# The last two transposes of a unit in the outputs' PSUM bank, in a fused attention and FFN block

## The reference

```python
x = L0_attn_hidden_states            # (4, 512, 1024)
xn = _layernorm(x, axis=-1)
x = x + attn(xn, w_qkv, w_o) + ffn(xn, W, b, A, B, gate_w, gate_b)

# attn: 32 query heads, 8 key/value heads, D = 128
scores = jnp.einsum('bqhgd,bkhd->bhgqk', q, k) * scale
bias = -slopes[:, :, None, None] * sqrt_dist          # -inf above the diagonal
attn = jax.nn.softmax(scores + bias[None], axis=-1)
out = jnp.einsum('bhgqk,bkhd->bqhgd', attn, v)
return out.reshape(B, S, NH * D) @ w_o
```

## Time and profile before

| | |
|---|---|
| median of 3 runs | 2472.68 us (2472.03 to 2477.65) |
| profiled execution, its own time | 2475.28 us |
| its span in the trace | 2473.4 us |
| PE busy | 2377.9 us (96%) |
| DVE busy | 1547.1 us (63%) |
| ACT busy | 1373.4 us (56%) |
| POOL busy | 784.2 us (32%) |
| granted TensorE clock, mean | 0.991 |

### The profile page before, as it was taken

The page is one execution under the profiler, slowest core; times in us unless marked ns, Lnnn a source line. Parts: engine busy times, 40 slices in busy tenths (PEclk is TensorE's granted clock), DMA queues, the critical chain, the costliest instruction groups (busy, mean ns, idle before and its releaser), DMA issues.

```text
span 2473.4 us, 34303 instructions
## 1 busy us (share of the span) xinstructions
PE 2377.9 (96%) x11616; PEld 1991.7 (81%) x11616; DVE 1547.1 (63%) x2969; ACT 1373.4 (56%) x3051; POOL 784.2 (32%) x1029
## 2 busy tenths in 40 slices
PE   5999999998799999999899999999999999999999
PEld 4787888887678788888778888788888888888887
DVE  5657355655655645555676666767667666676665
ACT  4532133334533223333477777777777777777774
POOL 3211000000330100000244645446455464554644
PEclk9999999999899999999999999999999999999999
DMA  4536445546254635445655565655655556666553
GB/s 151 182 129 209 146 146 184 191 170 236 71 175 157 207 120 204 153 170 196 235 185 182 188 230 203 208 194 188 226 201 210 198 188 218 201 211 206 187 175 141
DMA packets 118318, 455.90 MB, mean 184 GB/s; under 512 B 11945, under 2 KB 12089, under 8 KB 109184
## 3 DMA queue, kind: packets, MB, share of 16 engines
q1 hardware_dynamic: 86176, 334.37, 39.2%
q0 software_dynamic: 31968, 119.33, 13.9%
HBM read 276.96 MB, written 176.69 MB: 183 GB/s over the span
## 4 chain that ended last, share of the span: by engine, by line
PE 85%; DVE 5%; ACT 4%; issue 3%; DMA 3%; POOL 1%; SPq 0%; ACTq 0%; DVEq 0%; POOLq 0%
PE ps L677 26%; PE ps L678 26%; PE ps L679 26%; PE ps L877 5%; DMA lora_lo<-lora_s 1%; DMA qk_s<-res_b 1%; ACT probs L1085 1%; ACT res_hi L945 1%; DVE stats L1197 1%; DVE wo L1183 1%; ACT rows L974 1%; PE ps L857 1%; ACT probs L1107 1%; DVE w_lo L1183 0%; DMA qk_s<-res_hi 0%
## 5 line engine op out<-in xcount | busy, mean ns | idle before, releaser
L945 ACT ACTIVATE w_hi<-raw 128x1024 fp32r<-128x1024 f32 x196 | 207.0, 1059 | 558.9 <-PE ps L679 439.5
L1467 DVE TENSOR_TENSOR acc<-ps,acc 128x512 f32<-128x512 f32 x448 | 297.2, 686 | 287.3 <-issue 260.8
L1183 DVE TENSOR_TENSOR w_lo<-raw,w_hi 128x1024 fp32r<-128x1024 f32 x196 | 239.1, 1224 | 357.8 <-ACT w_hi L945 357.6
L677 PE MATMUL ps<-x_hi,w_hi 128*128 128x512 f32 x1120 | 436.5, 390 | 0.0
L678 PE MATMUL ps<-x_lo,w_hi 128*128 128x512 f32 x1120 | 436.0, 389 | 0.0
L679 PE MATMUL ps<-x_hi,w_lo 128*128 128x512 f32 x1120 | 435.9, 389 | 0.0
L1085 ACT ACTIVATE probs<-probs,neg_max 128x512 f32<-128x512 f32 (+3 forms) x512 | 283.9, 566 | 168.8 <-DVE neg_max L1432 168.8
L677 PE MATMUL ps<-wo,op_hi 128*128 128x512 f32 x896 | 363.5, 406 | 2.0 <-POOL op_lo L635 0.7
L678 PE MATMUL ps<-wo,op_hi 128*128 128x512 f32 x896 | 352.1, 393 | 0.0
L679 PE MATMUL ps<-wo,op_lo 128*128 128x512 f32 x896 | 351.5, 392 | 0.0
L679 PEld LDWEIGHTS ps<-x_hi,w_lo 128*128 128x128 f32 x1120 | 210.4, 188 | 43.9
(11 more groups left out here) (166 smaller groups left out, 4637.1 us busy)
## 6 DMA issues: line engine op xcount, KB each, us to landing
raw<-w_all SPq DMA_DIRECT2D x70, 1024.0 KB, 5.4
q<-qk_s SPq DMA_DIRECT2D x128, 512.0 KB, 3.9
acc<-acc_s SPq DMA_DIRECT2D x128, 512.0 KB, 5.1
acc_s<-acc SPq DMA_DIRECT2D x112, 512.0 KB, 7.7
qk_s<-res_hi POOLq DMA_DIRECT2D x40, 1024.0 KB, 4.6
qk_s<-res_a POOLq DMA_DIRECT2D x20, 1024.0 KB, 9.2
qk_s<-res_b POOLq DMA_DIRECT2D x20, 1024.0 KB, 5.2
k<-qk_s SPq DMA_DIRECT2D x32, 512.0 KB, 3.6
```

The lines of the kernel that those rows point to most:

```text
L677: pe.matmul(to, st_hi, mv_hi, start=start, stop=False, skip_group_check=True)
L945: nc.scalar.activation(to, source, ACT.Copy).then_inc(signal, 1)
L1183: nc.vector.tensor_tensor(to, source, high.bitcast(F32), ALU.subtract).then_inc(signal, 1)
L1467: nc.vector.tensor_tensor(to, fill[f % 2][:, :], to, ALU.add).then_inc(s_acc, 1)
```

## The change

The third group of transposes goes to `ps_o` instead of `ps_c`. The wait of that group for the maxima of the next unit's widest scores is taken out, and so is the wait of the widest scores for the copies of the transposes two units back. Nothing else differs; the same instructions run on every engine in the same order.

```diff
@@ -170,8 +170,7 @@
         score_rest = ps_a[:, P:2 * P]
         SCORES = (3, 2, 1, 0)
 
-
-        t_banks = [(ps_t0, 0, 512), (ps_t1, 512, 512), (ps_c, 1024, 256)]
+        t_banks = [(ps_t0, 0, 512), (ps_t1, 512, 512), (ps_o, 1024, 256)]
         o_banks = [ps_o, ps_t1]
 
         s_ident = sem("s_ident")
@@ -848,8 +847,6 @@
                 for c, i in enumerate((3, 2, 0, 1)):
                     if n and i != 1:
                         pe.wait_ge(s_neg_max, QT * (n - 1) + (c + 1 if i else 4))
-                    if n >= 2 and i == 3:
-                        pe.wait_ge(s_pt_lo, 3 * (n - 1))
                     cut, keys = slice(i * P, (i + 1) * P), slice(0, (i + 1) * P)
                     if i == 0:
 
@@ -871,8 +868,6 @@
                         [(0, i) for i in range(4)], [(1, 1), (1, 2), (1, 3), (3, 3)], [(2, 2), (2, 3)])):
                     if to is ps_t1 and n >= 2:
                         pe.wait_ge(s_at_raw, n // 2)
-                    if to is ps_c and n + 1 < UNITS:
-                        pe.wait_ge(s_neg_max, QT * (n + 1) + 1)
                     for c, (j, i) in enumerate(blocks):
                         last = pe.transpose(to[:, c * P:(c + 1) * P],
                                             probs[:, n % 2, OFF[i] + j * P:OFF[i] + (j + 1) * P], ident[:, :])
```

## The result

| | before | after |
|---|---|---|
| median of 8 runs each, us | 2473.52 (2471.59 to 2477.65) | 2480.91 (2479.24 to 2482.96) |
| ratio, 95% interval | | 1.0029 (1.0018 to 1.0040) |
| profiled execution, us | 2475.28 | 2480.64 |
| its span, us | 2473.4 | 2478.8 |
| mean granted clock of it | 0.991 | 0.989 |

The change made the kernel 7.4 us slower, clear of noise. The median lies over the range that was forecast (to 2477.5) and just under its bound of 0.3% for "slower".

What follows compares the result with a forecast made beforehand. PE, busy 96% of the span, was taken to bound the kernel, so only standing time could be gained. All parts were taken as 0: profiled 2475.3 us, median about 2472.5 us, range 2468.5 to 2477.5 us; no change got 0.93.

Steps and rivals of the forecast that it cites:

- its bound of 0.3% for "slower": Whole kernel: about 0.3%, 7.4 us, is what a measurement can tell from no change; slower than that got 0.04.
- Part one, the transposes' wait: Attention stage, ahead of the third group: wait removed, but the third fill still waits for DVE's addition; gain 0.
- The rival that gains 20.9 us: PE's attention-stage waits: both removed waits are gained whole, 19.1 + 1.8 us, giving 2451.8 us; chance 0.03.
- Part two, the scores' wait: Scores waiting for `pt_lo`, 1.79 us in step 6: the wait moves to that step's transposes; gain 0.
- Parts three and four, queue and bank: PE's queue: some 250 fewer waits, 0 to 2.5 us off, taken as 0; `ps_o` bank: over 3 us spare, cost 0.
- Part five, the clock: Turns of the output weights: joined waits could change clock falls, 1.22 us each; no change taken.
- possible better case: Turns of the output weights: the fill now ahead of the wait makes clock falls less frequent, 1.2 us faster.
- the worse one: Turns of the output weights: the joined 2.3 us wait brings up to 6 more clock falls, 7.3 us slower.
- the rival that had it: Turns of the output weights: the joined wait lets the clock fall at each, 2480 to 2490 us; chance 0.04.
- The argument against: Against the slower-clock rival: waits of 1.79 and 1.18 us within 7 us in step 6 brought no clock fall.

Runs made afterwards that it cites:

- the split run: Changed kernel, with PE waiting for the first maximum between the second fill's two products in steps with n % 16 == 6: 2475.89 us, ratio 1.0008.

## Why the prediction was wrong, point by point

- **Part one, the transposes' wait: right.** The third fill starts when it did in relation to the maxima (2.67 us both times); the wait became 1.05 us in the odd steps and 2.11 to 2.16 us in the even ones. The forecast was 1.22 and 2.30 us, reckoned from start to start; so reckoned, steps 37 and 38 of the changed kernel have 1.23 and 2.30 us. A turn without a fall takes 155.24 us after and 1713.68 - 1558.39 = 155.29 us before. The rival that gains 20.9 us is dead.
- **Part two, the scores' wait: right**, by the run that put it back (2480.95 beside 2480.91 us).
- **Parts three and four, queue and bank: right at 0.** The run with the new bank and only the transposes' wait put back equals the kernel before (1.0001, 0.9992 to 1.0010). So the new bank and one wait instruction fewer in each step cost and bring nothing that can be measured.
- **Part five, the clock: this is the step that failed.** The prediction had the mechanism and its price and wrote "I take no change": it took the total standing time as deciding and let a possible better case weigh against the worse one. The runs showed 5 falls at 7 turns in place of 1. The price was sized too low as well, 1.22 us against 1.44 us: it was read from the third fill alone, and in the changed kernel the slow stretch reaches into the outputs behind it. 0.04 was given to the rival that had it. Its lowest figure, 2480 us, is near the 2480.91 us measured by a different sum: it took a fall of 1.22 us at every turn, and there were five of seven, each dearer.
- What should have turned it: step 22 of the kernel before, one fall behind 1.82 us of waiting, said that the turns stood near the edge, and near an edge a change of the spacing need not be neutral. The argument against, that 1.79 and 1.18 us in step 6 brought no fall, spoke of pieces no longer than those that already were there, and not of one of over 2 us.
- The range left out its own rival. It took in three more falls of 1.2 us; five of seven at 1.44 us went past it.
- **The Trainium skill's rule.** The prediction cited the Trainium skill, "TensorE: Matmul & The Clock Gate", Part 4, that a transpose doesn't count as busy for the gate in the way a matmul does. By that rule it would have been 1.2 us faster. The runs don't bear it out: there were more falls, not fewer, and twenty-six transposes in a row, with 0.4 us of the 2.1 us of standing left behind the next fill, had the clock at 1.00 at every turn. Here they count for something, and with that the reason for the better case falls: in the kernel before, the wait was a piece of 1.8 us and not one of over 3 us with the transposes around it.

What stays open: why a fall comes at some turns and not at others of the same execution, and how standing time in two pieces adds up; the split run shows only that both happen. It is not shown either that the joining is the reason for the four falls more: the change made one piece longer and also moved it behind the second fill. The longest piece alone doesn't decide, since pieces of 0.93 and 0.96 us brought three falls where the kernel before, with one of 1.83 us, has one.

## What to carry to other kernels

When an edit only moves a wait on a TensorE that is the bound, the sum isn't zero by itself: look at the granted clock behind each place where it stands, and if one of several equal places already shows a fall, price the case in which all do. A wait that interrupts work early can be worth more than the same wait later in one longer piece; better still is to follow the wait to the engine that is late, here a 1.4 us split in DVE's order that had itself waited 1.8 us for ACT, and whose move gave 14 us. And a wait in the list is a gain only if what comes next isn't waiting for the same engine: the next signal of that engine tells.

## What the runs showed of the hardware

- One piece of 2.1 to 2.2 us without PE work in a dense stream was followed by the 1.2 GHz level for some 3.4 us at 5 of 7 places, in each of two kernels; one of 1.8 us at 1 of 7, in each of two kernels; two of 0.93 and 0.96 us at 3 of 7; one of some 1.43, 0.80 or 0.39 us at none. Each count is from one execution. A fall costs 1.2 to 1.5 us here.
- Sixteen more PE transposes of 128x128 float32 blocks, some 1.7 us of them, held the clock at 7 of 7 places, as 0.7 and 1.4 us of matmuls did.
- Extra matmuls and transposes, 3 to 16 of them in each of the turns, in time in which PE would stand anyway, cost nothing and made the changed kernel 7 to 9 us faster (2480.91 us to 2474.17, 2472.89 and 2472.24 us).
